# Both normalizations moved to ACT, biases of the normalizations on DVE, paddings issued by SP and ACT, result rows summed in three instructions

## What is computed

```
x = x + tanh(g_xattn) * attention(layernorm(x), ctx)   # 16 heads of 8, 77 context rows a sequence
x = x + tanh(g_ffn)   * ffn(layernorm(x))
attention: softmax(clip(q k^T / sqrt(8), +-10000)) v, then @ Wo + bo
ffn: scores = softmax(x router_w^T + bias); the 4 best of 32 experts, their scores normalized
     expert: silu(x gate_e^T) * (x up_e^T), then @ down_e^T, hidden size 128
     plus a shared expert of hidden size 512 on every token
layernorm: (x - mean) / sqrt(var + 1e-5), no weights
```

## Time and profile before

| what | value |
|---|---|
| median of 3 runs | 1083.81 us |
| the profiled execution | 1080.21 us |
| its span, first to last instruction | 1078.3 us |
| PE / DVE / ACT / POOL busy | 88% / 68% / 57% / 63% |
| mean granted TensorE clock | 0.976 of full speed |
| stage one, up to the last row scattered | 0 to 572 us |
| stage two | 592 to 995 us |
| stage three | 995 to 1078 us |

### The profile page before, as it was taken

The page is one execution under the profiler, slowest core; times in us unless marked ns, Lnnn a source line. Parts: engine busy times, 40 slices in busy tenths (PEclk is TensorE's granted clock), DMA queues, the critical chain, the costliest instruction groups (busy, mean ns, idle before and its releaser), DMA issues.

```text
span 1078.3 us, 26023 instructions
## 1 busy us (share of the span) xinstructions
PE 954.1 (88%) x6592; PEld 727.2 (67%) x6593; DVE 736.7 (68%) x2513; ACT 613.7 (57%) x2213; POOL 682.5 (63%) x947
## 2 busy tenths in 40 slices
PE   4998888888888988888868999999999999999976
PEld 2777777777777777777654766666676676766544
DVE  3788898898888988988755444444444444444796
ACT  3676677777667777777531555555555555554111
POOL 1276777777767777777666476777777777777000
PEclk9999999999999999999869899999999999999999
DMA  5511111111111111112213333333333333330893
GB/s 157 194 40 33 34 39 38 33 39 38 33 33 37 40 33 36 38 35 73 100 37 99 97 99 93 93 93 90 95 93 94 92 93 93 91 96 23 299 363 118
DMA packets 90278, 90.42 MB, mean 84 GB/s; under 512 B 21277, under 2 KB 71562, under 8 KB 89860
## 3 DMA queue, kind: packets, MB, share of 16 engines
q1 hardware_dynamic: 72452, 55.34, 18.0%
q0 software_dynamic: 17792, 34.67, 9.9%
HBM read 49.72 MB, written 42.31 MB: 85 GB/s over the span
## 4 chain that ended last, share of the span: by engine, by line
PE 43%; issue 16%; DVE 16%; DMA 12%; POOL 10%; ACT 1%; POOLq 1%; SPq 0%; DVEq 0%; ACTq 0%
PE ps L1072 11%; DMA x_rows<-payload,slot 11%; POOL x_rows L432 9%; PE ps L1083 9%; DVE payload L753 3%; PE ps L1109 3%; PE ps L1067 3%; PE ps L1077 3%; PE ps L1099 3%; PE ps L1093 3%; PE ps L1036 2%; DVE kvbd L679 2%; PE ps L1045 2%; PE ps L943 1%; DVE x_all L886 1%
## 5 line engine op out<-in xcount | busy, mean ns | idle before, releaser
L450 POOL DMA_INDIRECT y_rows<-y_sb,xin x288 | 283.1, 983 | 127.6 <-issue 81.9
L432 POOL DMA_INDIRECT x_rows<-payload,slot x256 | 251.2, 981 | 130.2 <-DVE slot L764 67.9
L839 DVE TENSOR_TENSOR h<-sg,ps 128x128 f32<-128x128 f32 x288 | 82.8, 288 | 183.7 <-ACT sg L577 183.7
L1072 PE MATMUL ps<-w_gu,xT 128*128 x576 | 175.7, 387 | 8.3 <-issue 8.3
L1083 PEld LDWEIGHTS ps<-w_dn,hT 128*128 128x128 f32 x576 | 94.3, 189 | 106.0 <-ACT hT L582 73.5
L943 PE MATMUL ps<-vt,pT 128*128 128x108 f32 x1024 | 146.1, 288 | 0.0
L943 PEld LDWEIGHTS ps<-vt,pT 128*128 128x128 f32 x1024 | 131.0, 200 | 11.6 <-issue 11.2
L582 ACT COPY hT<-ps 128x128 f32<-128x128 f32 x288 | 76.4, 265 | 109.6 <-PE ps L1077 107.9
L1083 PE MATMUL ps<-w_dn,hT 128*128 x576 | 129.9, 307 | 8.0 <-DVE y_sb L845 6.0
L577 ACT ACTIVATE sg<-ps 128x128 f32<-128x128 f32 x288 | 80.5, 279 | 72.7 <-PE ps L1072 48.6
L845 DVE TENSOR_SCALAR y_sb<-ps,xin 128x128 f32<-128x128 f32 x288 | 100.0, 347 | 24.1 <-PE ps L1083 22.5
(11 more groups left out here) (136 smaller groups left out, 2011.9 us busy)
## 6 DMA issues: line engine op xcount, KB each, us to landing
xin<-x_rows SPq DMA_DIRECT2D x288, 65.0 KB, 1.8
w_gu<-y_rows SPq DMA_DIRECT2D x16, 1024.0 KB, 7.7
y_rows<-y_sb,xin POOLq DMA_INDIRECT x288, 2.3
w_gu<-in_gu SPq DMA_DIRECT2D x2, 2048.0 KB, 9.6
x_rows<-payload,slot POOLq DMA_INDIRECT x256, 2.4
out<-x_all SPq DMA_DIRECT2D x16, 256.0 KB, 5.0
w_dn<-in_dn SPq DMA_DIRECT2D x1, 2048.0 KB, 8.5
ctx_sb<-in_ctxT SPq DMA_DIRECT2D x64, 29.2 KB
```

The source lines that it names most:

```text
L432: nc.gpsimd.indirect_dma_start(x_rows, bass.IndirectOffsetOnAxis(ap=slot[:, v, k:k + 1], axis=0), payload[:, v, k, :], None).then_inc(sent ...
L450: nc.gpsimd.indirect_dma_start(y_rows, bass.IndirectOffsetOnAxis(ap=xin[:, u, D:D + 1].bitcast(U32), axis=0), y_sb[:, u, :], None, bounds_ ...
L839: nc.vector.tensor_tensor(h[:, u % 2, :], sg[:, u % 2, :], ps_gu[u % 2][:, H:2 * H], ALU.mult).then_inc(h_d[u % PER], 1)
L1072: after(nc.tensor.matmul(ps_gu[u % 2][:, 0:2 * H], xT[:, u % 2, :], w_gu[:, bass.ds(e * (2 * H), 2 * H)], start=True, stop=True), xT_d, n, ...
```

## The change

- The first normalization leaves POOL. DVE computes `nb1 = -mean * rs1` (128x1) behind the residual add, and ACT writes `xn = rs1 * x + nb1` with one Identity between `relu(1)` and `vt`.
- The second normalization leaves DVE. DVE computes `nb2 = -mean * rs2` (128x1) in the place of the payload, and ACT writes the four copies with one Identity of 128x512 behind `vtail`. ACT, not DVE, now waits for `sent`.
- `relu_tails` of a block moves from the start of ACT's next step to behind the payload write. POOL's `prod` moves behind the token numbers. `idxf` goes; the one-hot comparison reads the integer indices.
- POOL issues no pads. SP issues 16 and ACT 16, two ahead of each of the first eight `ssilu`.
- `combine` adds the halves (128x1024), then the quarters (128x512), then into x (128x512): three instructions in place of four.

```diff
-PADS_SP = 20
+PADS_SP = 16
@@ SP
-                    sp.wait_ge(acc_d, TOPK * (c - 3))
+                    sp.wait_ge(acc_d, c - 3)
-                sp.wait_ge(acc_d, TOPK * (c + 1))
+                sp.wait_ge(acc_d, c + 1)
@@ POOL, step
-                    need(pool, rs1_d, m + 1)
-                    need(pool, xnT_p, m - 1)
-                    need_first(pool, xn_d, m)
-                    nc.gpsimd.tensor_tensor(xc[:, :], x_all[:, bass.ds(m * D, D)],
-                                            mv1[:, u, 0:1].broadcast_to([128, D]), ALU.subtract).then_inc(xc_d, 1)
-                    need(pool, xc_d, m + 1)
-                    nc.gpsimd.tensor_tensor(xn[:, u, :], xc[:, :], rs1[:, u:u + 1].broadcast_to([128, D]),
-                                            ALU.mult).then_inc(xn_d, 1)
...
-            for e in range(PADS_SP, E):
-                nc.gpsimd.indirect_dma_start(x_rows, bass.IndirectOffsetOnAxis(ap=padidx[:, e:e + 1], axis=0),
-                                             pad[:, :], None).then_inc(t_padded2, 16)
@@ ACT, step
+                if has(2):
+                    m = i + 2
+                    need(act, nb1_d, m + 1)
+                    need(act, xnT_p, m - 1)
+                    nc.scalar.activation(xn[:, u, :], x_all[:, bass.ds(m * D, D)], ACT.Identity, bias=nb1[:, u:u + 1],
+                                         scale=rs1[:, u:u + 1]).then_inc(xn_d, 1)
...
                 if has(-2):
+                    m = i - 2
+                    need(act, nb2_d, m + 1)
+                    need(act, sent[u], upto(m, u, 64))
+                    nc.scalar.activation(payload[:, u, :, 0:D],
+                                         x_all[:, bass.ds(m * D, D)].unsqueeze(1).broadcast_to([128, TOPK, D]),
+                                         ACT.Identity, bias=nb2[:, :], scale=rs2[:, :]).then_inc(x2_d, 1)
+                if has(0):
+                    relu_tails()
@@ ACT, first eight units of the shared expert
+            act.wait_ge(t_basei, 1)
             for n in range(4 * EARLY):
+                if n % 2 == 0:
+                    firsts = numbers(act, basei, PADS_SP + 2 * n, 4, XROWS - 128)
+                for first in firsts[2 * (n % 2):2 * (n % 2) + 2]:
+                    act.dma_start(x_rows[bass.ds(first, 128), :], pad[:, :]).then_inc(t_padded2, 16)
                 ssilu(n, n % 4)
@@ DVE, step
-                    nc.vector.tensor_copy(idxf[:, :], idx[:, 0:TOPK]).then_inc(idxf_d, 1)
...
+                    need(dve, rs1_d, m + 1)
+                    need(dve, xn_d, m - 1)
+                    nc.vector.tensor_scalar(nb1[:, u:u + 1], mv1[:, u, 0:1], -1.0, rs1[:, u:u + 1], ALU.mult,
+                                            ALU.mult).then_inc(nb1_d, 1)
...
-                    need(dve, sent[u], upto(m, u, 64))
-                    nc.vector.tensor_scalar(payload[:, u, :, 0:D], xi.unsqueeze(1).broadcast_to([128, TOPK, D]),
-                                            mv2[:, 0:1], rs2[:, :], ALU.subtract, ALU.mult).then_inc(x2_d, 1)
+                    need(dve, x2_d, m)
+                    nc.vector.tensor_scalar(nb2[:, :], mv2[:, 0:1], -1.0, rs2[:, :], ALU.mult,
+                                            ALU.mult).then_inc(nb2_d, 1)
@@ DVE, combine
-                for k in range(TOPK):
-                    if k:
-                        dve.wait_ge(acc_d, TOPK * c + k)
-                    nc.vector.tensor_tensor(xs, xs, yld[:, c % 4, :, k, :], ALU.add).then_inc(acc_d, 1)
+                two, one = yld[:, c % 4, :, 0:2, :], yld[:, c % 4, :, 0, :]
+                nc.vector.tensor_tensor(two, two, yld[:, c % 4, :, 2:4, :], ALU.add).then_inc(half_d, 1)
+                dve.wait_ge(half_d, 2 * c + 1)
+                nc.vector.tensor_tensor(one, one, yld[:, c % 4, :, 1, :], ALU.add).then_inc(half_d, 1)
+                dve.wait_ge(half_d, 2 * c + 2)
+                nc.vector.tensor_tensor(xs, xs, one, ALU.add).then_inc(acc_d, 1)
```

More of the change, by code:

```diff
@@ L111, in build @@
         rs1 = sb("rs1", [128, 2])
-        xc = sb("xc", [128, D])
+        nb1 = sb("nb1", [128, 2])
+        nb2 = sb("nb2", [128, 1])
         xn = sb("xn", [128, 2, D])
@@ L135, in build @@
         idx = sb("idx", [128, 8], U32)
-        idxf = sb("idxf", [128, TOPK])
         onehot = sb("onehot", [128, TOPK, E], BF16)
@@ L163, in build @@
         basei = sb("basei", [1, E], I32)
-        padidx = sb("padidx", [128, E], U32)
         tab_sb = sb("tab_sb", [1, TG * TW], I32)
@@ L222, in build @@
         passed = sem("passed")
+        half_d = sem("half_d")
         def need_first(eng, s, count):
@@ L400, in step @@
                 if has(0):
-                    need_first(pool, xn_d, i + 1)
+                    need(pool, xn_d, i + 1)
                     xi = x_all[:, bass.ds(i * D, D)]
                     nc.gpsimd.tensor_tensor(xi, xi, bias2[:, :], ALU.add).then_inc(xb_d, 1)
-                if has(2):
-                    m = i + 2
-                    need(pool, rs1_d, m + 1)
-                    need(pool, xnT_p, m - 1)
-                    need_first(pool, xn_d, m)
-                    nc.gpsimd.tensor_tensor(xc[:, :], x_all[:, bass.ds(m * D, D)],
-                                            mv1[:, u, 0:1].broadcast_to([128, D]), ALU.subtract).then_inc(xc_d, 1)
-                    need(pool, xc_d, m + 1)
-                    nc.gpsimd.tensor_tensor(xn[:, u, :], xc[:, :], rs1[:, u:u + 1].broadcast_to([128, D]),
-                                            ALU.mult).then_inc(xn_d, 1)
                 if has(-3):
                     m, v = i - 3, o
[L418 to L421, removed]
                     need(pool, sent[v], upto(m, v, 64))
@@ L429, in step @@
                                             ALU.add).then_inc(dest_d, 1)
+                    need(pool, pos_d, m + 1)
+                    nc.gpsimd.tensor_tensor(prod[:, :, :], onehot[:, :, :],
+                                            pos[:, :].unsqueeze(1).broadcast_to([128, TOPK, E]),
+                                            ALU.mult).then_inc(prod_d, 1)
                     need_first(pool, slot_d, m + 1)
@@ L478, in relu_tails @@
                 def relu_tails():
-                    need(act, diff_d, 2 * i)
+                    need(act, diff_d, 2 * i + 2)
                     need(act, pt_p, FILLS * (i - 1))
-                    nc.scalar.activation(ptail[:, o, :, 0:TAIL], prob[:, o, :, 128 * CH:GK], ACT.Relu,
+                    nc.scalar.activation(ptail[:, u, :, 0:TAIL], prob[:, u, :, 128 * CH:GK], ACT.Relu,
                                          scale=-1.0).then_inc(relu_d, 1)
@@ L489, in fill @@
                                          scale=-1.0).then_inc(pt_d, 1)
-                if has(-1):
-                    relu_tails()
                 if has(2):
@@ L526, in step @@
                     need(act, mv2_d, i - 1)
-                    need(act, x2_d, i - 2)
+                    need(act, nb2_d, i - 2)
                     nc.scalar.activation(lv2[:, :], mv2[:, 1:2], ACT.Ln, bias=eps[:, :]).then_inc(lv2_d, 1)
@@ L547, in step @@
                 if has(-2):
+                    m = i - 2
[6 more added lines that the diff above has]
+                    relu_tails()
+                if has(-2):
                     need(act, x2T_p, i - 1)
@@ L696, in step @@
                     maxima(1)
-                if has(-3):
-                    need(dve, idx_d, i - 2)
-                    nc.vector.tensor_copy(idxf[:, :], idx[:, 0:TOPK]).then_inc(idxf_d, 1)
                 if has(0):
@@ L705, in step @@
                     m = i - 3
-                    need(dve, idxf_d, m + 1)
+                    need(dve, idx_d, m + 1)
                     need(dve, pre_p, m)
                     nc.vector.tensor_tensor(onehot[:, :, :], iota.unsqueeze(1).broadcast_to([128, TOPK, E]),
-                                            idxf[:, :].unsqueeze(2).broadcast_to([128, TOPK, E]),
+                                            idx[:, 0:TOPK].unsqueeze(2).broadcast_to([128, TOPK, E]),
                                             ALU.is_equal).then_inc(oh_d, 1)
@@ L795, in _ @@
             nc.vector.tensor_copy(basei[:, :], base[0:1, B % 2, :]).then_inc(t_basei, 1)
-            nc.vector.tensor_scalar(padidx[:, :], last, cst[:, C_P:C_P + 1], None, ALU.add).then_inc(t_padidx, 1)
             link(nc.vector.tensor_tensor(cnt[:, :], last, cst[:, C_EOFF:C_EOFF + E], ALU.subtract))
```

20 lines of the change are left out of this document (9 added, 11 removed).

## The result

The changed kernel takes 1130.22 us (median of 4 runs, 1122.05 to 1135.45) beside 1084.28 for the one before: ratio 1.041, 95% interval 1.036 to 1.046. I had forecast 1086.5 in a range of 1074 to 1099. The profile is of the execution of 1135.45 us, the slowest of the four, 55.2 more than the one profiled before; sums made from its rows are compared with that. The medians differ by 45.9.

The account below looks back on a forecast made before the run. Stage one was taken as bound by a ring of waits through scatters, payload and `slot`, 8.14 us a step. Terms +7.0 - 2.0 + 0.5 - 2.8 = +2.7 on 1080.21 gave 1082.9, as median 1086.5; range 1074 to 1099.

Parts of the forecast that it names:

- The ring is cut, and a wait on PE takes its place: Stage one: waits from scatters through payload to `slot`, 8.14 us a step, end; PE waits for payload, delaying `keys_values`.
- Loops of 8.25: Stage one: two loops of waits within 0.05 us of each other set the step at 8.25 us.
- Loop B: Stage one, loop of waits through DVE from `kvbd` to the next: 7.38 + P a step.
- A: Stage one, loop of waits through PE: 7.43 + P, 8.24 us a step, taken as the longer loop.
- P: Duration of ACT's payload instruction in stage one: 0.81 us, bounds 0.63 and 0.95.
- The clock falls as often as before: Stage one: four clock falls cost the same 5.2 us, the slow clock at the end 1.6.
- the total of idle time stays: Stage one: argument against more clock falls, that PE's idle time is split in two but keeps its sum.
- the rival: Stage one: clock falls more often, 15 steps instead of 4 paying 1.3 us each, +14, 1101 us; chance 0.12.
- Behind the last `kvbd`, -2.0: End of stage one: in the four draining steps the last scatters go earlier, -2.0 us, bounds -3 and 0.
- between the stages, +0.5: Between stages: ACT's last pads land at 589.3 instead of 588.84, +0.5 us, bounds -1.5 and +1.5.
- Three sums, -2.8: Stage three: three adds instead of four save 0.19 us a chunk over 15 chunks, -2.8 us.
- The much faster case: Stage one: payload not in the loop, POOL's 7.65 or the old remainder 7.4 rules, 33 us less, 1050; chance 0.08.

Follow-up runs that it names:

- e1: Changed kernel with PE's keys_values moved ahead of the transposition of payload; ratio 0.998 to the kernel before.
- e3: Changed kernel with constants 0 and 1 as bias and scale of ACT's payload, leaving out the second normalization; ratio 1.009 to the kernel before.
- e6: Kernel of e4 with two unused 128x128 additions on POOL ahead of the first scatter, so scatters start later; ratio 1.013 to the kernel before.
- e5: Kernel of e1 with ACT's order changed: payload right behind relu(1), then vt and vtail, then xn; ratio 1.001 to the kernel before.
- e4: Changed kernel with six useless identity transpositions on PE ahead of the transposition of payload; ratio 1.023 to the kernel before.
- e8: Kernel before with the three-instruction sum alone; ratio 0.998 to the kernel before.
- e10: Changed kernel with payload and relu_tails put back, slotf, gate and slot ahead of payload, prod ahead of token numbers; 1036.86 us, ratio 0.960 to the kernel before.
- e11: Kernel before with DVE's slotf, gate and slot ahead of payload and nothing else; ratio 0.983 to the kernel before.
- e9: Kernel before with only the second normalization moved to ACT (payload with nb2, relu_tails behind it); ratio 1.045 to the kernel before.

## Why the prediction was wrong

- *The ring is cut, and a wait on PE takes its place.* Right. L981 waits for ACT's payload 63 times, `kvbd` for L963, and e1, which takes the keys and values out of that queue, gives the loss back.
- *Loops of 8.25.* The step that failed. Loop B is the longer, not A (`vt` starts 0.29 behind PE's last context matmul, since `xn` runs first), and takes 8.68 in the step shown and 8.71 on average where I put 7.38 + P = 8.19. P was right: 0.81, and 0.63 with constants (e3). Mis-sized were `kvbd` to `relu(1)`, 5.31 (295.14 to 300.45; 5.32 on average) for 4.93, and `vt` to payload, 0.70 for 0.60. By the averages of the quiet steps the first was 5.06 before, so the 4.97 that I read in one step was 0.09 short. The removed `idxf` had stood beside a wait and its going gave nothing: the clamp starts 2.35 behind `kvbd` in both kernels. The rest of the way from 5.06 to 5.32 is the clamp, 0.43 for 0.18, and 0.09 where `nb1` now stands, less 0.05 behind it. e6 gave 0.19 of the clamp's part back. The payload starts 0.02 behind the end of `vtail` where I had put 0.09 ahead of it; behind `relu(1)`, in e5, it does start ahead, and the runs do not show why it doesn't here. 8.71 for 8.25 is 0.46 x 60 = 28 us of the miss.
- *The clock falls as often as before.* Wrong: 25 long steps for 3, and 32.5 us above the quiet pace where I had 6.8 (5.2 + 1.6): 26 us of the miss, which is 60.3 - 7.0 = 53 for the profiled execution; by the medians it is 44. (The 0.79 of the earlier trace rows is the mean of a window that holds one fall to half the clock.) I held "the total of idle time stays" against the rival; it did not stay. PE's wait per step in 60 to 540 us rose from 1.05 to 1.34 us, with 1.19 in e3, and the granted clock fell 5, 22 and 6 times there. e4 and e6, which fill the wait, leave about 0.5 us and no fall, so the idle time is the cause and not only its companion. But its sum alone does not give the number: e1 has 5 falls at 0.54 us. Before, PE had 15 waits of over 1.2 us, and each fall came within 3 us of one of them; in the changed kernel none is over 1.15 us, and regular waits of 1.1 in every step brought more falls. The rival had the mechanism at 15 steps and a chance of 0.12.
- *Behind the last `kvbd`, -2.0; between the stages, +0.5.* The drain gave nothing (the last scatter of stage one starts 39.61 us behind the last `kvbd`, before 39.57), while the last pad landed 1.4 earlier. With stage two 1.0 shorter, which no edit explains, the rest of the kernel gave 5.0 where I had 4.3: near, but by chance.
- *Three sums, -2.8.* Right within the uncertainty of e8; 3.1 in the trace of the changed kernel.
- *The much faster case* (POOL's round as the limit) was no outcome of this change, and POOL's round was not the limit in e10 either, but e10 shows that the room was there: it had the payload on DVE and `slot` ahead of it.

## What to carry to other kernels

When a wait holds an engine, look first at which instructions behind it do not need its result: moving three small ones ahead gained 1.7% (e11), and 4.0% together with the rest of the change and an earlier `prod` (e10), while moving the waiting instruction to another engine lost 4.5% (e9). Before moving work to an engine, go round every loop that passes through it, with the instruction in each. And where a change adds to PE's waiting, price the clock as well: 0.18 us less on ACT was worth 3.2% here (e3), about half of it through the clock.

## What the runs showed of the hardware

- A VectorE `tensor_scalar` of 128x16 between SBUF tiles took 0.17 us, but was held up by an indirect DMA on GpSimd (0.96 us busy) that had begun before it: in the first three of a block when it started 0.53 to 0.76 us behind the DMA's start (49 of 49, up to 0.40 us), in the last from about 0.3 us on (up to 0.64), and up to 1.16 us where it also outlasted the addition behind. Earlier or later starts, 241 in the first three, were free. That the two engines share a port would explain it and was not measured. The Trainium skill (SBUF — State Buffer, Who interferes with whom) has such a pair of ports, locked by one engine for a whole instruction. The waiting agrees with it; that a DMA of 0.96 us holds the clamp in a part of its time only does not follow from it.
- An ACT instruction of 128x512 took 631 ns with constants and 814 with two per-partition operands, 183 more for both. With the 0.09 us of a bias in the earlier trace rows, that leaves as much for the scale.
- The granted clock between 60 and 540 us was 0.92 in the changed kernel, where PE waited in pieces of about 1.1 and 0.3 us in each step and was busy the rest of it, and 1.00 in e4, where most of the first piece was filled.
